# After the edge stages of a graph network: aggregate in channel rows, per-partition polynomial weights, features left in PSUM, attention output inside the edge stage

## The reference

```python
xn = _layernorm(x)
# graph part: C = 64; h0 = xn[:, :64], h1 = the other 192 channels as (64, 3)
m0e = tpw0*x0*sh0 + tpw3*einsum(x1, sh1)/sqrt3;  m1e = tpw1*x0*sh1 + tpw2*x1*sh0   # per edge
msg0, msg1 = segment_sum(m0e, dst), segment_sum(m1e, dst)
A0 = msg0 @ W_lin0;  A1 = msg1 @ W_lin1;  vv = sum(A1*A1, -1)
B0 = Wc0[:,0]*A0 + Wc0[:,1]*A0**2 + Wc0[:,2]*vv + Wc0[:,3]*A0**3 + Wc0[:,4]*A0*vv
B1 = (Wc1[:,0] + Wc1[:,1]*A0 + Wc1[:,2]*A0**2 + Wc1[:,3]*vv)[..., None] * A1
o0 = B0 @ WB0 + h0 @ Wsc0;  o1 = B1 @ WB1 + h1 @ Wsc1
# then o0 is normalised over the nodes (mean, variance), o1 by its mean square over the nodes
# attention part, 8 heads of 64, linear: K and V normalised per head
out = q @ (K^T V) / n;  mix = out @ Wout^T + bout
x = x + graph + mix
# ffn: w = layernorm(x) @ wr + br; the 999 best nodes get w * (gelu(xn @ w1 + b1) @ w2 + b2) added; all get xn + x
```

## Time and profile before

| | us |
|---|---|
| median of three runs | 1653.01 |
| the profiled execution, its own time | 1646.3 |
| its span | 1644.5 |
| mean granted TensorE clock | 0.894 |
| TensorE, VectorE, GpSimd, ScalarE busy | 1313.0, 961.9, 957.1, 572.2 |

### The profile page before, as it was taken

The page is one execution under the profiler, slowest core; times in us unless marked ns, Lnnn a source line. Parts: engine busy times, 40 slices in busy tenths (PEclk is TensorE's granted clock), DMA queues, the critical chain, the costliest instruction groups (busy, mean ns, idle before and its releaser), DMA issues.

```text
span 1644.5 us, 39777 instructions
## 1 busy us (share of the span) xinstructions
PE 1313.0 (80%) x13447; PEld 788.2 (48%) x13447; DVE 961.9 (58%) x2519; ACT 572.2 (35%) x1849; POOL 957.1 (58%) x1008
## 2 busy tenths in 40 slices
PE   3587877878878778585788988888888888865999
PEld 2354545545545545344444444444444445534467
DVE  5445545555443444355676767676767767586753
ACT  3233333333333333134243434343434333333420
POOL 0777777777777777302677777777777777300000
PEclk9678889888798898687899999999999999987999
DMA  6433333333332332032333333333333333200001
GB/s 214 111 74 83 79 79 85 76 80 80 78 83 74 80 85 73 15 143 89 92 111 113 109 113 113 113 112 109 113 108 113 110 110 114 67 0 0 1 13 37
DMA packets 79036, 141.96 MB, mean 86 GB/s; under 512 B 25562, under 2 KB 34170, under 8 KB 78328
## 3 DMA queue, kind: packets, MB, share of 16 engines
q0 software_dynamic: 40128, 81.99, 18.9%
q1 hardware_dynamic: 38712, 57.46, 11.5%
HBM read 134.69 MB, written 4.67 MB: 85 GB/s over the span
## 4 chain that ended last, share of the span: by engine, by line
PE 36%; POOL 18%; DVE 18%; issue 17%; DMA 5%; DVEq 3%; ACT 2%; SPq 0%; POOLq 0%; PEldq 0%; ACTq 0%
POOL ring L420 18%; DVE arena L1381 6%; PE ps L967 4%; PE ps L953 4%; PE ps L940 4%; PE ps L989 4%; DMA ring<-mtab,src 4%; PE ps L1113 3%; PE ps L1104 3%; DVE arena L1379 3%; DVE arena L1371 3%; PE ps L783 2%; PE ps L701 1%; PE ps L976 1%; DVE small L1133 1%
## 5 line engine op out<-in xcount | busy, mean ns | idle before, releaser
L430 POOL DMA_INDIRECT arena<-utab,src x500 | 474.6, 949 | 259.2 <-issue 147.3
L420 POOL DMA_INDIRECT ring<-mtab,src x500 | 480.3, 961 | 196.9 <-issue 188.0
L1243 DVE TENSOR_TENSOR arena<-ps,ring 128x1024 f32<-128x1024 f32 x125 | 153.0, 1224 | 283.7 <-PE ps L783 278.3
L1381 DVE TENSOR_TENSOR arena<-ps,arena 128x768 f32<-128x768 f32 x252 | 228.2, 947 | 0.0
L582 ACT ACTIVATE arena<-ps 128x512 f32<-128x512 f32 x195 | 117.0, 600 | 314.9 <-PE ps L940 309.9
L953 PE MATMUL ps<-arena 64*128 64x256 f32 x1016 | 151.9, 419 | 87.9 <-DVE arena L1381 87.9
L967 PE MATMUL ps<-arena 128*8 128x256 f32 x4032 | 170.5, 313 | 0.0
L783 PE MATMUL ps<-arena,ring 128*64 128x128 f32 x2000 | 162.5, 313 | 0.0
L1371 DVE TENSOR_TENSOR arena<-arena,ps 128x16 f32 x512 | 87.1, 170 | 124.2 <-PE ps L976 66.0
L774 PE MATMUL ps<-ring 128*32 128x97 f32 x1000 | 50.8, 278 | 125.8 <-DMA ring<-mtab,src 125.4
L953 PEld LDWEIGHTS ps<-arena 64*128 64x128 f32 x1016 | 91.6, 193 | 122.1 <-issue 76.7
(11 more groups left out here) (226 smaller groups left out, 1840.5 us busy)
## 6 DMA issues: line engine op xcount, KB each, us to landing
arena<-in_eaT SPq DMA_DIRECT2D x125, 256.0 KB
ring<-mtab,src POOLq DMA_INDIRECT x500
arena<-utab,src POOLq DMA_INDIRECT x500
arena<-in_rbf SPq DMA_DIRECT2D x132, 32.0 KB
ring<-in_fw SPq DMA_DIRECT2D x2, 1024.0 KB, 5.7
utab<-arena SPq DMA_DIRECT2D x4, 512.0 KB, 4.1
XT<-in_xT SPq DMA_DIRECT2D x2, 1000.0 KB
out<-XT SPq DMA_DIRECT2D x15, 128.0 KB, 1.7
```

The costliest lines, as they stand in the source:

```text
L420: pool.indirect_dma_start(MR[:, n % 4, k, 0:H], None, mtab, bass.IndirectOffsetOnAxis(ap=src[:, 4 * n + k:4 * n + k + 1], axis=0)).then_in ...
L430: pool.indirect_dma_start(G1[:, n % NSLOT, k, :], None, utab, bass.IndirectOffsetOnAxis(ap=src[:, 4 * n + k:4 * n + k + 1], axis=0)).then_ ...
L1243: dve.tensor_tensor(RM[:, n % 2, :, :, :], ps[:, 1, 0:P].rearrange("p (t q) -> p t q", t=4).unsqueeze(3).broadcast_to([P, 4, KH, WIN]), SW ...
L1381: return dve.tensor_tensor(q[:, :, 3 * part - 2:3 * part + 1, :], tp[:, :, part + 1:part + 2, :].broadcast_to([P, 4, 3, H]), x[:, :, 1:4, ...
```

## The change: what it does, and the diff

- **Stage length.** NQ = 125: the empty quad, with its placeholder DMAs, is gone, and the last odd half of the octet loop is skipped.
- **Attention schedule.** `mix1` takes 5 quads a tile (MT1) in place of 7: K at f = 0 on TensorE and ScalarE, V and its squares at f = 1, norms at f = 2 and 3, K^T V at f = 2, scaling of V at f = 4. The final matrices follow at quads 84 to 89. The attention output (8 blocks of two 128 x 512 matmuls) runs at quads 92, 96, ..., 120; one quad later VectorE adds bias and `XT` while it takes each block out of PSUM.
- **Aggregate in channel rows.** A is made channels in rows, 500 nodes at a time, by 64 x 64 matmuls in all four quarters of the array, so that A0 of two node ranges fills 128 partitions of a bank. The polynomial reads it from PSUM; its weights are one value per partition, applied by ScalarE as scale and bias and by VectorE in `scalar_tensor_tensor`. No transposes back.
- **Features left in PSUM.** B times WB is accumulated on the self connection in the banks that held A; statistics read PSUM; ScalarE applies scale and shift while it copies; VectorE adds that to Y1.
- **Scores.** VectorE multiplies the normalised rows by `wr` with a running sum; 16 transposes of a broadcast column make the repeated row, placed after the fourth of the 32 feed-forward blocks.

```diff
-NQ = ROUNDS * QR
-NO = NQ // 2
+NQ = ET // 4
+NO = -(-NQ // 2)
+MT1 = 5
+Y1AT = [MT1 * NT + 12 + 4 * i for i in range(8)]
...
@@ tensor: mix1
-                t, f = divmod(n, 7)
+                t, f = divmod(n, MT1)
-                if t < NT and f in (0, 2):
+                if t < NT and f in (0, 1):
-                if 1 <= t <= NT and f == 1:
+                if 1 <= t <= NT and f == 2:
...
+                if n in Y1AT:
+                    i = Y1AT.index(n)
+                    c, o = divmod(i, 2)
+                    pe.wait_ge(S["s_Gm1"], j + 1)
+                    if i >= 2:
+                        pe.wait_ge(S["s_y1e"], j * 8 + i - 1)
+                    for k in range(2):
+                        mm = pe.matmul(ps[:, 6 + i % 2, :], GM1[:, k, o * P:(o + 1) * P], YT[:, k, 512 * c:512 * c + 512],
+                                       start=(k == 0), stop=(k == 1))
+                    mm.then_inc(S["s_y1"], 1)
@@ tensor: after the edge stage
+            for q in range(2):
+                for p in range(2):
+                    for h in range(2):
+                        for r in range(2):
+                            mm = pe.matmul(ps[half(h), 4 * q + 2 * p + r, 0:NCH], wl[half(r), p, half(r)],
+                                           acc1[half(r), p, span_of(h, q)], start=True, stop=True)
+                    mm.then_inc(S["s_ar"], 1)
+            for q in range(2):
+                pe.wait_ge(S["s_b"], q + 1)
+                for k in range(2):
+                    for h in range(2):
+                        pe.matmul(ps[:, 4 * q + 2 * h + k, 0:NCH], bds[:, k, :], YT[:, k, span_of(h, q)],
+                                  start=True, stop=False, skip_group_check=True)
+                    for r in range(2):
+                        for h in range(2):
+                            mm = pe.matmul(ps[half(r), 4 * q + 2 * h + k, 0:NCH], bdb[half(h), min(2 * k + r, 1), :],
+                                           BC[half(h), 2 * k + r, q * NCH:(q + 1) * NCH], start=False, stop=True,
+                                           skip_group_check=True)
+                    mm.then_inc(S["s_o"], 1)
...
@@ tensor: feed-forward
+                if i == 4:
+                    pe.wait_ge(col[3], 8)
+                    pe.wait_ge(S["s_wcol"], 1)
+                    for t in range(NT):
+                        tr = pe.transpose(ps[:, t // 4, t % 4 * P:(t % 4 + 1) * P],
+                                          wcol[:, t:t + 1].broadcast_to([P, P]), ident)
@@ scalar: mix1
-                if t < NT and f == 1:
+                if t < NT and f == 0:
...
-                if t < NT and f == 3:
+                if t < NT and f == 1:
...
-                if t < NT and f == 6:
+                if t < NT and f == 4:
@@ scalar: after the edge stage
+            for q in range(2):
+                act.wait_ge(S["s_w4"], 16 * NLOAD["s_w4"])
+                act.wait_ge(S["s_ar"], 2 * q + 1)
+                a0 = ps[:, 4 * q, 0:NCH]
+                act.activation(SQA[:, q, 0, :], a0, ACT.Square).then_inc(S["s_are"], 1)
+                act.activation(LIN[:, q, 0, :], a0, ACT.Identity, bias=wc[:, 0:1], scale=wc[:, 1:2]).then_inc(S["s_are"], 1)
+                act.activation(LIN[:, q, 1, :], a0, ACT.Identity, bias=wc[:, 5:6], scale=wc[:, 6:7]).then_inc(S["s_are"], 1)
+                for b in range(1, 4):
+                    act.wait_ge(S["s_ar"], 2 * q + 1 + b // 2)
+                    act.activation(SQA[:, q, b, :], ps[:, 4 * q + b, 0:NCH], ACT.Square).then_inc(S["s_are"], 1)
+            act.wait_ge(S["s_nr"], 2)
+            for c in range(4):
+                h, q = divmod(c, 2)
+                for k in range(2):
+                    act.activation(OT[:, k, c * NCH:(c + 1) * NCH], ps[:, 4 * q + 2 * h + k, 0:NCH], ACT.Identity,
+                                   bias=obi[:, k:k + 1], scale=osc[:, k:k + 1]).then_inc(S["s_oe"], 1)
@@ vector: mix1
-                    if t < NT and f == 4:
+                    if t < NT and f == 2:
...
+                    if n - 1 in Y1AT:
+                        dve.wait_ge(S["s_y1"], j * 8 + i + 1)
+                        dve.scalar_tensor_tensor(Y1[:, o, 512 * c:512 * c + 512], ps[:, 6 + i % 2, :], boc[:, o:o + 1],
+                                                 XT[:, o, 512 * c:512 * c + 512], ALU.add, ALU.add
+                                                 ).then_inc(S["s_y1e"], 1)
@@ vector: after the edge stage
+            for q in range(2):
+                dve.wait_ge(S["s_are"], 6 * q + 3)
+                dve.scalar_tensor_tensor(u, q0, wc[:, 3:4], u, ALU.mult, ALU.add)
+                dve.scalar_tensor_tensor(v, q0, wc[:, 7:8], v, ALU.mult, ALU.add)
+                dve.wait_ge(S["s_are"], 6 * q + 5)
+                link(dve.tensor_tensor(vv, q1, q2, ALU.add))
+                dve.wait_ge(S["s_are"], 6 * q + 6)
+                link(dve.tensor_tensor(vv, vv, q3, ALU.add))
+                link(dve.scalar_tensor_tensor(v, vv, wc[:, 8:9], v, ALU.mult, ALU.add))
+                dve.scalar_tensor_tensor(u, vv, wc[:, 4:5], u, ALU.mult, ALU.add).then_inc(S["s_bt"], 1)
+                for x in range(3):
+                    dve.tensor_tensor(BC[:, 1 + x, nodes], a[1 + x], v, ALU.mult)
+                dve.wait_ge(S["s_bt"], 2 * q + 1)
+                dve.tensor_tensor(tp, a[0], u, ALU.mult).then_inc(S["s_bt"], 1)
+                dve.wait_ge(S["s_bt"], 2 * q + 2)
+                dve.scalar_tensor_tensor(BC[:, 0, nodes], vv, wc[:, 2:3], tp, ALU.mult, ALU.add).then_inc(S["s_b"], 1)
+            for q in range(2):
+                for k in range(2):
+                    dve.wait_ge(S["s_o"], 2 * q + k + 1)
+                    for h in range(2):
+                        ins = dve.bn_stats(sto[:, k, 2 * h + q, :], ps[:, 4 * q + 2 * h + k, 0:NCH])
...
+            for c in range(4):
+                dve.wait_ge(S["s_oe"], 2 * c + 2)
+                for k in range(2):
+                    nodes = slice(c * NCH, (c + 1) * NCH)
+                    ins = dve.tensor_tensor(XT[:, k, nodes], Y1[:, k, nodes], OT[:, k, nodes], ALU.add)
+                ins.then_inc(xtd[3], 1)
             layer_norm(3)
+            for t in range(NT):
+                dve.wait_ge(lny[3], t + 1)
+                ins = dve.scalar_tensor_tensor(OUTR[:, t, :], YROW[:, t, :], 1.0, wrr, ALU.mult,
+                                               ALU.mult, accum_out=wcol[:, t:t + 1])
```

More of the change, by code:

```diff
@@ L244, in build @@
         shv = r3.take(ETP * 4).rearrange("p (t k) -> p t k", k=4)
[L247 to L252, removed]
+        SQA = arena[:, 8192:8192 + 8 * NCH].rearrange("p (q b n) -> p q b n", q=2, b=4)
+        LIN = arena[:, 23552:23552 + 4 * NCH].rearrange("p (q v n) -> p q v n", q=2, v=2)
+        VV = arena[:, 25600:25600 + 2 * NCH].rearrange("p (q n) -> p q n", q=2)
+        TP = ring[:, 6720:6720 + 2 * NCH].rearrange("p (q n) -> p q n", q=2)
+        BC = arena[:, 26752:26752 + 8 * NCH].rearrange("p (b n) -> p b n", b=4)
+        Y1 = cols(19456)
+        OT = cols(12288)
         HT = cols(12320, 8)
@@ L637, in _ @@
                     silu(j, 3 * o + 7, 1)
-                    collect(j, 2 * o + 1, 1)
+                    if 2 * o + 1 < NQ:
+                        collect(j, 2 * o + 1, 1)
                     silu(j, 3 * o + 8, 0)
                     mix1(j, 2 * o + 1)
[L641 to L644, removed]
@@ L1038, in _ @@
             pe.wait_ge(S["s_w4"], 16 * NLOAD["s_w4"])
-            for i in range(NT // 2):
-                if i >= 4:
-                    pe.wait_ge(S["s_are"], i - 3)
-                for t in range(2):
-                    for h in range(NA):
-                        mm = pe.matmul(ps[:, 4 + i % 4, t * D + h * P:t * D + (h + 1) * P],
-                                       acc1[:, h, (2 * i + t) * P:(2 * i + t + 1) * P], wl[:, h, :], start=True, stop=True)
-                mm.then_inc(S["s_ar"], 1)
@@ L1060, in _ @@
-            pe.wait_ge(S["s_Gm1"], npass)
-            for i in range(8):
-                c, o = divmod(i, 2)
-                pe.wait_ge(S["s_are"], i + 5) if i < 4 else pe.wait_ge(S["s_y1e"], i - 3)
-                for k in range(2):
-                    mm = pe.matmul(ps[:, 4 + i % 4, :], GM1[:, k, o * P:(o + 1) * P], YT[:, k, 512 * c:512 * c + 512],
-                                   start=(k == 0), stop=(k == 1))
-                mm.then_inc(S["s_y1"], 1)
-            for i in range(4, 8):
-                back(i)
@@ L1070, in _, with half @@
-            for i in range(8):
-                c, k = divmod(i, 2)
-                pe.wait_ge(S["s_bte"], i + 1)
-                pe.wait_ge(S["s_oe"], i - 3) if i >= 4 else pe.wait_ge(S["s_y1e"], i + 5)
-                pe.matmul(ps[:, 4 + i % 4, :], bdb[:, k, :], BT[:, k, 512 * c:512 * c + 512], start=True, stop=False)
-                pe.matmul(ps[:, 4 + i % 4, :], bds[:, k, :], YT[:, k, 512 * c:512 * c + 512], start=False,
-                          stop=True).then_inc(S["s_o"], 1)
+            def half(c):
```

(14 more changed lines are left out.)

191 lines of the change are left out of this document (55 added, 136 removed).

## The result

The changed kernel takes 1622.28 us in the median of four runs (1620.77 to 1622.48), the kernel before 1649.62 us beside it (1645.87 to 1653.49): a ratio of 0.9832, 95% interval 0.9801 to 0.9863, 27.3 us less. The profiled execution took 1622.41 us with a span of 1620.6 us (before: 1646.3 and 1644.5), at a mean granted clock of 0.898. The forecast was 1616 us.

| stretch | before | after | after minus before | forecast of that |
|---|---|---|---|---|
| span's start to aggregate product | 1430.53 | 1454.08 | +23.55 | +13.3 |
| aggregate product to layer-norm transposes | 73.38 | 34.70 | -38.7 | -38.9 |
| transposes to the span's end | 140.6 | 131.8 | -8.8 | -7.7 |
| sum | 1644.5 | 1620.6 | -23.9 | -33.3 |

A forecast was written before the change was run, and what follows sets the result against it. The edge stage was taken as set narrowly by the TensorE-VectorE loop (5.12 us a quad), GpSimd (5.0) just behind, then a serial chain. +13.3 - 38.9 - 7.7 = -33.3 gave 1613.0 or 1619.7; middle 1616, range 1590 to 1638.

The forecast's parts named there:

- 1. Five quads a tile: Second edge stage, quads 0 to 80: 27.15 us a tile, 434.4 for 16 tiles, so quad 80 starts 26 us later.
- the surcharge: Second edge stage: attention work costs 6.95 us a tile beyond the bare quads of 4.13 us each.
- Rival B: Attention tiles: waits for ScalarE's K and V batches make a tile 30.9 us, the whole 1676 us; chance 0.07.
- 2. Quads 80 to 124: Rest of the edge stage: GpSimd's gathers set the pace, 214.7 us, and hide the attention output, quad 124 at 1433.7.
- The other side of my bound: Quads 80 to 124: the loop alone would need 205 us, bare quads 182, final matrices 7.7, attention-output blocks 15.
- rival A: Edge stage: GpSimd was the pace all along and hides the denser mix; quad 124 at 1402, about 1585 us; chance 0.12.
- Step 4: Aggregate product to layer-norm transposes: 34.5 us in place of 73.4, a saving of 38.9 us.
- step 5: Layer-norm transposes to the end: scores made beside four feed-forward blocks, last stage at 1578.0 in place of 1585.75, saving 7.7 us.
- 3. End of the stage: Quad 124 to the aggregate product: 10.2 us in place of 10.8, aggregate product at 1443.9, 13.3 us later than before.
- Rival C: After the edge stage: low clock in all products, slower ScalarE passes and late scores add 9 us, 1625 us; chance 0.16.

## Why the prediction was right, and where it was off

**1. Five quads a tile: right in kind, 6.2 us too small.** Forecast 27.15 us a tile; measured (1225.17 - 785.32) / 16 = 27.49, and the stage started 0.8 later. The first tile alone takes 30.80 (quad 0 at 785.32, quad 5 at 816.12). The other fifteen take 27.27 on average, 0.12 over the forecast: eight take 26.75 to 26.95 and seven 27.6 to 27.85. In or at the edge of each of the seven the granted clock falls for about 3.4 us, but it also falls in three of the eight quick ones, so a fall alone doesn't make a slow tile. Two windows of the kernel after, the first such a fall (span, then busy time and count of PE, PEld, DVE, ACT, POOL, granted clock, DMA share, GB/s):

```profile
1222.80:1226.20 3.40, 3.34 (x20) 1.62 (x24) 1.92 (x7) 0.13 (x1) 1.13 (x2) 0.51 0.32 98
1464.70:1468.40 3.70, 3.67 (x8) 1.22 (x8) 3.60 (x6) 0.00 (x0) 0.00 (x0) 0.50 0.00 0
```

The number of these falls doesn't explain the miss. Between 795 and 1120 us there are nine in the kernel after (one of them in the first tile) and eight in the kernel before, so the surcharge that I read from the earlier trace rows already held them. Of the 5.4 us that sixteen tiles took beyond the forecast, 3.65 lie in the first. In this tile the granted clock was 0.50 to about 793 us, as in the kernel before, and it fell to 0.50 again from about 806 to 813, beginning in a wait of TensorE of 3.51 us for VectorE; the kernel before has no second such stretch there. Its own first tile took 37.28, 1.4 over its mean of 35.86. My sum of one mean tile had no term for the start; how the rest of the 3.65 divides is open. The range of 26.5 to 28.0 held the mean. VectorE's wait for ScalarE's squares ahead of the norms, forecast at 0.5 on even tiles or 4 us in all, came to 1.4 us in all. Two rows carry the wrong quad: 1402.85 and 1406.98 are quads 121 and 122, not 122 and 123. The step of 4.13 between them is that of a quad without attention work all the same, but four such steps, 1402.85 to 1419.69, average 4.21. Rival B, ScalarE's batches on the path at 30.9 a tile, did not happen.

**2. Quads 80 to 124: the mechanism right, 4.1 us too small.** Forecast 214.7 us from quad 80 to quad 124, measured 218.8, paced by GpSimd with VectorE waiting for the landing. Of the difference, 2.0 lies in the start: from quad 80 to the first gather of quad 83 were 1230.36 - 1225.17 = 5.2 us in place of 3.2, because GpSimd stood still for 2.13 us ahead of the gather at 1226.60, the second of quad 82. That is no accident of this run: the same gather has the same stand in the kernel before, at 1195.03,

```profile
1195.03 0.94 POOL L430 DMA_INDIRECT arena<-utab,src  x1 [1.99 <-issue]
```

and in the kernel after the second gathers of quads 28 and 55 also come late (2.55 and 2.98 us after the first, in place of 1.25), each 27 quads from the next. With five slots these places are quads 28, 53 and 78. So the stand belongs to a place in GpSimd's list; what it is the profile doesn't show. The forecast could have had it from the trace before. Of the rest of the difference, 1.7 lies in the pace: 167 steps of 1.26 us, where I had read 1.25 from seven. What is left is the last landing (2.2 in place of 1.8). The other side of my bound, 205 us for the loop alone, was not measured. The 205.8 with the lead of five look like it, but are GpSimd's pace again: VectorE still waits 8.1 us for gathers in them, and without the blocks, with some 15 us less to do in the loop by my estimate, the stretch is no shorter (206.5). The nearest measure of the loop is six quads a tile with the lead of five, which has no wait for gathers: 134.6 us from quad 96 to quad 124 (1298.29 to 1432.92), where the same sum, 28 x 4.13 + 7.7 + 15, gives 138.3. So the loop's side of the bound was 4 us too high, or nearer 201 (an estimate from these two). The blocks were free, as forecast, and rival A (GpSimd the pace all along, quad 124 near 1402) did not happen: GpSimd was held for 45.1 us before quad 80 (16.7 us in the kernel before, in the same 785 to 1225 us), and quad 124 came at 1443.93.

Steps 1 and 2 together are **the term that was mis-sized**: the aggregate product comes 23.55 us later than before, not 13.3. That is 10.2 us too little. Step 4 adds 0.2 and step 5 gives 1.1 back, so the sum of -33.3 was 9.4 us too low against the trace; taking 1616 over the sum's 1613 left a miss of 6.3. The 3 us by which the forecast lies nearer than its sum are owed to that choice of a middle, not to the mechanism.

**3. End of the stage.** From quad 124 to the aggregate product 1454.08 - 1443.93 = 10.15 us, forecast 10.2.

**4. After the stage: right, 34.70 us against 34.5.** The errors in it nearly cancel. The polynomial was quicker than forecast: two halves of 7.27 us in place of 7.6, ending at 17.8 in place of 18.3. The first full product set ran at half clock, 3.70 us in place of 1.87, the second window above; TensorE had stood 5.37 us ahead of it. It was all but hidden: the second half of the polynomial came at 1471.9, and TensorE reached its products at 1472.40. ScalarE's eight passes took 5.39 us, 0.67 each, where I had 0.55: its passes with a scale and a bias cost more than its copies. Against that, the stretch from the end of the statistics to the first of these passes took 3.75 us where I had taken over 4.55: the small product of the statistics took 1.05 us where it had been 1.87. Rival C's low clock through all products did not come: only the first of four sets was slow.

The product sets also show what a change of tiling costs. In the chain above full-width L1064 and quarter-width L1068 alternate without idle time: 1469.53 + 1.87 = 1471.40, + 1.00 = 1472.40. The Trainium skill (TensorEngine Tiling (Array Packing), Tiling Modes, Key Properties) says that changing the mode drains the array. The trace agrees, and gives the size. In the kernel before, where the same full-width products follow each other without a change of tiling, two records of 512 columns take 0.86 us (start, duration, what, from its chain):

```profile
1473.60 0.86 PE ps L1074 x2
1474.46 0.86 PE ps L1075 x2
```

Four records of 500 columns would take 1.68; between two changes they took 1.87. That is 0.2 us more for each pair of sets, about 0.1 for each change. The bound that I had put on eight changes, 0.8 us, was what they cost, and my sum of 2.67 us a pair left it out: a pair took 2.87. That the change causes it is read from these rows, and no run takes the changes away.

**5. Scores: 8.8 us against 7.7.** The kernel before took 140.6 us from the layer-norm transposes to the end, this one 131.8. The surplus of 1.1 is not the scores'. From the layer-norm transposes to the next large product were 17.29 us before (1503.91 to 1521.20) and 16.19 now (1488.78 to 1504.97), a part that I had taken to be the same; from there to the last stage were 64.55 and are 56.69, a saving of 7.9 against the 7.7; the last stage is 0.2 longer. The 16 products with running sum on VectorE come every 0.345 us, not 0.52 (timeline of the kernel after, the first of them and the instruction behind the last):

```profile
1503.62 0.41 DVE L1491 SCALAR_TENSOR_TENSOR XT<-arena,ring 128x256 f32<-128x256 f32 x1
...
1509.26 0.23 DVE L1494 TENSOR_SCALAR small<-small 128x16 f32<-128x16 f32 x1
```

They are ready at 1509.5, 2.3 us ahead of the fourth block's end at 1511.84. The 2 us by which the fifth block was to come late are the transposes themselves, and they took 1.75.

**The best version** is the changed kernel with the lead of five quads: 1610.75 us, 0.9769 of the kernel before, 0.9748 to 0.9789, which lies clear of the change's 0.9801 to 0.9863. Seven quads a tile with the lead of five was not run; nor was a longer lead than five, so how much of the 26 us of squeezing a lead can win back at most is open. Open are also what delays the first tile beyond its low clock, and the cause of GpSimd's stand of 2.13 us.

## What to carry to other kernels

When work is squeezed into fewer iterations of a pipelined loop, the iterations get longer, and a queue with a short lead (here GpSimd's gathers) idles in them; what it didn't do there it owes later, when the loop is faster than it. Look at both halves: who waits for whom in the dense part, and who waits for whom after it. Before moving work to make room, lengthen the lead of the engine that issues the transfers; it is cheap in code. It must be the wait that changes, not only the number of buffers: here the buffers alone gave 1.3 us, which is within the intervals, and the wait with them 11.5. And compare with the work left uncompressed: with the output blocks behind the stage in both, seven quads a tile was 26 us faster than five.

## What the runs showed of the hardware that was not expected

- In the edge stage TensorE's granted clock falls to 0.50, its 1.2 GHz level, for about 3.4 us every 24 to 58 us, although TensorE is busy 375.29 of the 439.00 us from 785 to 1224 (85%). It happens in both kernels. Ahead of the window at 1222.8 TensorE had waited 1.76 and 2.01 us for VectorE. Seven tiles with or beside such a fall take about 0.9 us longer than the quick ones, three with a fall (at 837, 946 and 1110 us) don't.
- The same 32 records of the attention output took 14.03 us in the kernel before, 17.04 and 15.70 us where they stood ahead of the aggregate product, at the head of the work after the stage, with the granted clock at 0.50 at their start; 16 transposes took 1.75 us behind running products and 3.48 us after a wait of 4.55.
- VectorE's product with a running sum over 128x256 came each 0.345 us, though a single one lasts 0.41 to 0.42: one starts before the one ahead has ended. The price of 0.52 that I took from L1525 was that of another operation.
- Between two changes of tiling four full-width records of 500 columns took 1.87 us, where 1.68 follows from the kernel before (0.86 for two of 512), so about 0.1 us a change.
- GpSimd stands still for 0.7 to 2.1 us ahead of the second gather of certain quads: 28, 82 and 109 in the kernel before, 28, 55, 82 and 109 in the kernel after, all multiples of 27 quads apart, and 28, 53 and 78 in the changed kernel with five slots.
